# Attention decoder: second-pass scores in pairs of PSUM banks, first-pass scores in a ring of two banks

## The reference, cut to what matters

```python
scores = jnp.einsum('bhqd,bhkd->bhqk', q, k) / math.sqrt(HD)
scores = scores + mask[None]
attn = jax.nn.softmax(scores, axis=-1)
out = jnp.einsum('bhqk,bhkd->bhqd', attn, v)
```

## Time and profile before

| | us |
|---|---|
| median of 3 runs | 2834.61 (2833.82 to 2835.52) |
| the profiled execution's own time | 2834.0 |
| its span in the profile | 2832.2 |
| PE busy in the span | 2383.4 (84%) |
| DVE busy | 1830.1 (65%) |
| ACT busy | 1364.2 (48%) |
| GpSimd busy | 512.9 (18%) |
| mean granted clock of TensorE | 0.906 |

### The profile page before, as it was taken

The page is one execution under the profiler, slowest core; times in us unless marked ns, Lnnn a source line. Parts: engine busy times, 40 slices in busy tenths (PEclk is TensorE's granted clock), DMA queues, the critical chain, the costliest instruction groups (busy, mean ns, idle before and its releaser), DMA issues. The chain is left out here.

```text
span 2832.2 us, 37728 instructions
## 1 busy us (share of the span) xinstructions
PE 2383.4 (84%) x12692; PEld 999.5 (35%) x12692; DVE 1830.1 (65%) x4370; ACT 1364.2 (48%) x2333; POOL 512.9 (18%) x603
## 2 busy tenths in 40 slices
PE   6799999999999999999678798984556987999638
PEld 4333334343434434333243323431122533333215
DVE  3686777777776777777237765358999145877242
ACT  2365666666666666666535123344222612566420
POOL 1211111110111111010014001006896002100000
PEclk7799999999999999999889898986899986999868
DMA  2221222221222222121010000003332012222020
GB/s 91 83 90 43 81 66 69 74 82 53 70 65 79 69 66 81 50 71 54 20 36 1 22 1 27 0 12 120 126 138 100 23 44 69 83 64 74 20 90 15
DMA packets 77451, 171.60 MB, mean 61 GB/s; under 512 B 23049, under 2 KB 38665, under 8 KB 73163
## 3 DMA queue, kind: packets, MB, share of 16 engines
q1 hardware_dynamic: 77258, 169.18, 18.8%
HBM read 128.41 MB, written 39.71 MB: 59 GB/s over the span
## 5 line engine op out<-in xcount | busy, mean ns | idle before, releaser
L1056 ACT ACTIVATE sb_prob<-ps 128x512 f32<-128x512 f32 (+1 forms) x1520 | 805.3, 575 | 483.4 <-PE ps L846 307.9
L820 PE MATMUL ps<-sb_k_stack_half,sb_q_stack_half 78*128 78x512 bf16 (+3 forms) x1920 | 588.1, 340 | 56.2 <-DMA sb_q_stack_half<-q_rows 24.5
L846 PE MATMUL ps<-sb_q_stack_half,sb_k_stack_half 81*128 81x128 bf16 (+2 forms) x2240 | 569.8, 312 | 53.4 <-ACT sb_prob L1056 51.9
L957 DVE TENSOR_REDUCE sb_row_max<-ps 128x1 f32<-128x512 f32 x640 | 431.7, 686 | 140.6 <-PE ps L820 138.8
L966 DVE CUSTOM_DVE_ANT_0 sb_masked_scores<-ps,sb_mask_row,sb_row_max 128x128 bf16<-128x128 f32 (+3 forms) x640 | 341.2, 544 | 93.3 <-PE ps L820 90.0
L966 DVE CUSTOM_DVE_ANT_0 sb_masked_scores<-ps,sb_mask_row 128x128 bf16<-128x128 f32 (+3 forms) x640 | 283.2, 487 | 172.1 <-PE ps L820 171.3
L846 PEld LDWEIGHTS ps<-sb_q_stack_half,sb_k_stack_half 81*128 81x128 bf16 x2240 | 201.8, 99 | 385.6 <-ACT sb_prob L1056 199.2
L867 PE MATMUL ps<-sb_prob,sb_v_first_half 128*9 128x512 f32 (+3 forms) x2560 | 300.3, 542 | 0.2 <-ACT sb_o_raw L1063 0.2
L820 PEld LDWEIGHTS ps<-sb_k_stack_half,sb_q_stack_half 78*128 78x128 bf16 x1920 | 184.4, 100 | 268.7 <-DVE sb_row_max L966 79.4
L2606 PE MATMUL ps<-sb_read_out,sb_ident 128*128 128x512 f32 x256 | 139.6, 678 | 119.7 <-DVE sb_read_out L2693 113.8
L2660 POOL TENSOR_TENSOR sb_inflow<-sb_delta_u,sb_b_spread 128x1024 f32<-128x1024 f32 x64 | 201.4, 3162 | 26.3 <-DVE sb_states L2682 19.0
(11 more groups left out here) (375 smaller groups left out, 3171.6 us busy)
## 6 DMA issues: line engine op xcount, KB each, us to landing
sb_q_stack_half<-q_rows SPq DMA_DIRECT2D x240, 96.0 KB
sb_k_stack_half<-k_rows SPq DMA_DIRECT2D x40, 576.0 KB
o_rows<-sb_o_raw SPq DMA_DIRECT2D x80, 256.0 KB, 2.3
sb_b_spread<-b_rows SPq DMA_DIRECT2D x32, 512.0 KB, 4.7
sb_c_spread<-c_rows SPq DMA_DIRECT2D x32, 512.0 KB, 3.5
sb_k_stack_half<-k_rows SPq DMA_DIRECT2D x40, 288.0 KB
q_rows<-sb_qk_parts SPq DMA_DIRECT2D x60, 128.0 KB, 2.1
k_rows<-sb_qk_parts SPq DMA_DIRECT2D x60, 128.0 KB, 2.1
```

The lines of the kernel that those rows point to most:

```text
L820: pe.matmul(M.ps[:, k % RING, 0:hi - lo], qst[half][0:S1_ROWS, s, j, at:at + P], kst[half][0:S1_ROWS, s, lo // CH, j, 0:hi - lo], start=Tr ...
L846: mm = pe.matmul(bank[:, x * w + lo:x * w + hi], kst[half][0:S2_ROWS, s, t // 4, j, t % 4 * P:(t % 4 + 1) * P], qst[half][0:S2_ROWS, s, j, ...
L957: dve.reduce_max(rowmax[:, tau % 3, 0, at:at + 1], M.ps[:, k % RING, 0:w], AX_X).then_inc(first_done, 1)
L1056: act.activation(prob[:, st % PROB_STEPS, heads[0]:heads[-1] + 1, a:CH], scores.rearrange("p (j q) -> p j q", j=len(heads)), ACT.Exp).then ...
```

## The change

Units are now 2 heads at widths 512 and 384, and 4 heads at 256 and 128. A unit has two banks: one head in each at 512 and 384, two heads in each at 256; at 128 all four lie in the first bank. The second pass has two such pairs, banks 2 and 3, and 4 and 5. The first pass has the two banks 0 and 1. Both rings are now two deep (`RING` is 2). One ACT instruction exponentiates a whole unit.

PE computes a unit head by head, and the pieces that are due are put between the heads, with a mark for each head from `Plan`. The wait for the pair of banks stands before the unit's first head; the signal to ACT comes from its last matmul. A narrow head is one matmul of its whole width, where it was cut into matmuls of 128 columns, and the mask comes after a bank's heads, no longer before them.

```diff
--- before.py
+++ after.py
@@ -382,7 +382,7 @@
     def units_of(self, tau, t):
         half = self.tasks[tau][2]
         width = CH - max(t * P - half * CH, 0)
-        per = {2 * P: 2, P: 4}.get(width, 1)
+        per = 2 if width > 2 * P else 4
         return [tuple(range(j, j + per)) for j in range(0, GROUP, per)], width
 
     def side_items(self, q):
@@ -454,7 +454,7 @@
                 ready[q] = end + items[q][at[q]][1]
             return name, q, norm_of.get(q)
 
-        self.steps = []
+        self.steps, self.marks = [], {}
         now = 0.0
 
         def add(task=None, t=None, units=(), first=(0, 0), cost=0.0):
@@ -507,8 +507,12 @@
             units, width = self.units_of(tau, t)
             lo, rows = k, []
             for u in units:
-                done += (len(u) * width + self.DVE_FIX) / per_group
-                k = target(done)
+                marks = []
+                for _ in u:
+                    done += (width + self.DVE_FIX / len(u)) / per_group
+                    k = target(done)
+                    marks.append(k)
+                self.marks[(tau, t, u)] = marks
                 rows.append(("exp", tau, u, k))
                 rows += [("turn", x[1], None, k) for x in due_turns(k)]
             mask = 0.06 * GROUP if width < CH or t == 4 * self.tasks[tau][2] else 0.0
@@ -637,7 +641,7 @@
     plan = Plan(F.layers, F.ffn, F.rotate, SLOTS)
     col = F.col
     steps, tasks = plan.steps, plan.tasks
-    S2_BANK, RING, O_BANK, SIDE = 3, 3, 6, 7
+    S2_BANK, RING, O_BANK, SIDE = 2, 2, 6, 7
     ROWS = 4 * GROUP
 
     with ExitStack() as tmp:
@@ -825,31 +829,28 @@
                     pe.wait_ge(max_split, plan.splits[tau])
                     if v >= RING:
                         pe.wait_ge(unit_done, v - RING + 1)
-                    pe.matmul(M.ps[0:3 * ROWS, S2_BANK + v % RING, 0:P], m3[:, tau % 2].rearrange("p c r -> p (c r)"),
+                    pe.matmul(M.ps[0:3 * ROWS, S2_BANK + 2 * (v % RING), 0:P], m3[:, tau % 2].rearrange("p c r -> p (c r)"),
                               M.identb[:], start=True, stop=True).then_inc(s2_ready, 1)
 
-                def second(v, tau, t, heads):
+                def second(v, tau, t, heads, x):
                     half, s = tasks[tau][2], plan.slot[tau]
-                    if t == 0 and heads[0] == 0:
+                    if t == 0 and heads[x] == 0:
                         pe.wait_ge(rows_in[half][s], 48 * (plan.use[tau] + 1))
-                    if v >= RING:
+                    if v >= RING and x == 0:
                         pe.wait_ge(unit_done, v - RING + 1)
                     a, w, diag = place(tau, t)
-                    n = len(heads)
-                    bank = M.ps[:, S2_BANK + v % RING, 0:n * w]
-                    if n > 1:
-                        pe.matmul(bank.rearrange("p (j q) -> p j q", j=n)[:, :, 0:P], M.identb[:],
-                                  M.mask_kq[:].unsqueeze(1).to_broadcast([P, n, P]), start=True, stop=False)
-                    for x, j in enumerate(heads):
-                        for lo in range(0, w, P if n > 1 else w):
-                            hi = lo + (P if n > 1 else w)
-                            mm = pe.matmul(bank[:, x * w + lo:x * w + hi], 
-                                           kst[half][0:S2_ROWS, s, t // 4, j, t % 4 * P:(t % 4 + 1) * P],
-                                           qst[half][0:S2_ROWS, s, j, a + lo:a + hi], start=n == 1,
-                                           stop=x == n - 1 and hi == w and (n > 1 or not diag))
-                    if n == 1 and diag:
-                        mm = pe.matmul(bank[:, 0:P], M.identb[:], M.mask_kq[:], start=False, stop=True)
-                    mm.then_inc(s2_ready, 1)
+                    per = CH // w
+                    at, pos = divmod(x, per)
+                    bank = M.ps[:, S2_BANK + 2 * (v % RING) + at, 0:per * w]
+                    mm = pe.matmul(bank[:, pos * w:(pos + 1) * w],
+                                   kst[half][0:S2_ROWS, s, t // 4, heads[x], t % 4 * P:(t % 4 + 1) * P],
+                                   qst[half][0:S2_ROWS, s, heads[x], a:CH], start=pos == 0,
+                                   stop=pos == per - 1 and not diag)
+                    if diag and pos == per - 1:
+                        mm = pe.matmul(bank.rearrange("p (j q) -> p j q", j=per)[:, :, 0:P], M.identb[:],
+                                       M.mask_kq[:].unsqueeze(1).to_broadcast([P, per, P]), start=False, stop=True)
+                    if x == len(heads) - 1:
+                        mm.then_inc(s2_ready, 1)
 
                 def weigh(tau, t):
                     l, b, half, g = tasks[tau]
@@ -925,7 +926,11 @@
                         if kind == "turn":
                             turn(step["units_at"] + x, tau)
                         else:
-                            second(step["units_at"] + x, tau, step["t"], heads)
+                            for y, mark in enumerate(plan.marks[(tau, step["t"], heads)]):
+                                second(step["units_at"] + x, tau, step["t"], heads, y)
+                                while k < mark:
+                                    first(k)
+                                    k += 1
                         while k < upto and step["task"] is not None:
                             first(k)
                             k += 1
@@ -1043,7 +1048,7 @@
                     if tau >= 2:
                         half = tasks[tau - 2][2]
                         act.wait_ge(rows_in[half][plan.slot[tau - 2]], 48 * (plan.use[tau - 2] + 1))
-                    act.activation(turned[:, tau % 2, :], M.ps[0:3 * ROWS, S2_BANK + v % RING, 0:P],
+                    act.activation(turned[:, tau % 2, :], M.ps[0:3 * ROWS, S2_BANK + 2 * (v % RING), 0:P],
                                    ACT.Copy).then_inc(unit_done, 1)
 
                 def weight(v, tau, t, heads):
@@ -1052,9 +1057,15 @@
                     act.wait_ge(s2_ready, v + 1)
                     if heads[0] == 0 and st >= PROB_STEPS:
                         act.wait_ge(pv_done, st - PROB_STEPS + 1)
-                    scores = M.ps[:, S2_BANK + v % RING, 0:len(heads) * w]
-                    act.activation(prob[:, st % PROB_STEPS, heads[0]:heads[-1] + 1, a:CH],
-                                   scores.rearrange("p (j q) -> p j q", j=len(heads)), ACT.Exp).then_inc(unit_done, 1)
+                    bank = S2_BANK + 2 * (v % RING)
+                    if w > 2 * P:
+                        scores = M.ps[:, bank:bank + 2, 0:w]
+                    elif w == 2 * P:
+                        scores = M.ps[:, bank:bank + 2, :].rearrange("p k (j q) -> p (k j) q", j=2)
+                    else:
+                        scores = M.ps[:, bank, :].rearrange("p (j q) -> p j q", j=4)
+                    act.activation(prob[:, st % PROB_STEPS, heads[0]:heads[-1] + 1, a:CH], scores,
+                                   ACT.Exp).then_inc(unit_done, 1)
 
                 def save(tau):
                     act.wait_ge(pv_done, plan.step_index[(tau, plan.kbs[tau] - 1)] + 1)
```

## The result

The changed kernel takes 3013.6 us (median of 4 runs, 2990.5 to 3024.1) against 2834.2 us (4 runs, 2828.1 to 2835.5): **1.062 times as long**, 95% interval 1.058 to 1.067. The profiled execution took 3008.8 us, with a span of 3007.0 where that of before was 2832.2.

The account below looks back on a forecast made before the run. PE, busy 92% of the decoder stages, was taken to set the pace. The terms +175 + 10 + 8 - 28 = +165 us on 2834.0 gave 2999, rounded to 3000 us; the 8-in-10 range was 2880 to 3085.

Parts of the forecast that it names:

- Part 1: First pass: with two banks, a piece waits for DVE's end of piece k-2 instead of k-3; +175 us in all.
- The walk: Three first-pass steps of 512 queries worked through with the new waits for DVE: 1.90 us lost, 0.63 each.
- ACT's pairs: Second-pass exps: one per pair saves ACT 36 us, all beside its idle time, so the program gains 0 us.
- The turn: Second pass: at 19 of 80 turns the pair directly behind waits for the exp of the pair ahead; +10 us.
- `save`: Second step of a task: `weigh` waits for the later copy of sums in 27 of 80 tasks, 0.3 us each; +8 us.
- GELU: Block 0: PE's stops while ACT does GELU shorten at 14 places by 2.0 us each; -28 us.
- The lower end of part 1: Rival: the first pass's order self-corrects and its shorter ring costs only +80 us, total 2904 us; chance 0.15.
- the faster case: Rival: exps set the pace, DVE's delay is absorbed and PE's second-pass waits go, total 2770 us; chance 0.10.
- The clock rival: Rival: many short waits make TensorE's granted clock fall oftener, 70 us more, total 3070 us; chance 0.10.
- The signals: Profile after: idle before pieces up over 100 us, 800 exps, `weigh` inside GELU gaps, time outside decoders within 3 us.

Follow-up runs that it names:

- 2 / 3 kernel: Kernel before with the first-pass ring cut from three banks to two, the second pass keeping three single banks: 3042.1 us, ratio 1.071.
- four singles: Kernel before with two banks for the first pass and four single banks for the second, no pairs: 2998.4 us, ratio 1.056.
- the copies: GELU replaced by a plain copy, in the kernel before (2809.6 us, 0.991) and in the changed kernel (2978.2 us, 1.050).
- half the reducing: DVE reduces half of each first-pass piece and exp has scale 0, in the kernel before (2783.7 us, 0.981) and the changed kernel (2877.2 us, 1.013).

## Why the prediction was right, and where it wasn't

The direction and the size hold: 3013.6 us lie 14 above the forecast of 3000, and +179 us stand against a sum of +165. Point by point:

- **Part 1, +175 us.** The mechanism is shown by the 2 / 3 kernel, in which nothing but this ring is shorter. It lost 202 us (186 to 216), so the term was some 27 us short. The walk's waits came out at 0.61, 1.16, 0.08 and 0.39 us for 0.62, 1.07, 0.07 and 0.32. (The walk lets DVE take P8 at 712.08, though by its own numbers P8 lands at 711.76 + 0.33 + 0.04 = 712.13; with that it gives 0.37.) Its size over the whole program is not separated cleanly from the clock. The stages' 172 us hold both: at a granted clock c the share 2(1 - c) of the time runs at the lower level and at most half of that is lost, so block 0 lost at most 101 us after (0.07 x 1444) and 53 before (0.04 x 1315), block 3 39 and 25. Up to 62 us of the 172 can so be the clock's, and 110 to 172 are waits and what they bring. At the lower end of that the walk's 0.63 us did not arise in each of the 228 steps; the runs don't say in which. Without GELU block 0 grew by 116 us (1278 to 1394) at 0.97 in both kernels, so there next to nothing of the loss is the clock's.
- **ACT's pairs, 0 us.** The time of the exps fell by 59 us (805.3 to 746.5), 36 forecast, all of ACT's by 45, and the program's by none of it: four singles in the same banks take no longer. The Trainium skill (Perfetto Trace Analysis, Optimizing Scalar/DVE Operations) says that larger operations can pay if the engine is saturated. The trace agrees: ACT is busy in 54% of block 0's stage, and the pairs pay nothing.
- **The turn, +10 us.** The 19 turns with a pair directly behind them show 10.4 us of waits for exps, added up from the timeline, 0.1 to 0.85 each.
- **`save`, +8 us.** `weigh` waited for it 3 times, not 27, 1.9 us in all, and moving it gave 6 us within the scatter. It was priced too high; the runs don't say which of its lengths was off.
- **GELU, -28 us.** This is the step that failed: "so 2.3 us are won", added to part 1 as if the two were independent. At the stop they are won (1.03 us of wait for 2.78). Against the 2 / 3 kernel, which has the short first ring and the old second one, the change is 28 us faster and four singles are 44 us faster. Against the kernel before nothing is left: the copies show a net gain of none, or a loss of some 9 us. Both fit if GELU costs more once the first ring is short, and the clock says so. By the same bound GELU's share of low clock in block 0 costs at most 59 us after the change (0.07 x 1444 less 0.03 x 1394) and 15 before it. The 2 / 3 kernel without GELU, which would part the two, was not run. The forecast allowed for "the clock may still fall during the shorter stop" and took 0.3 us for it.
- **The rivals.** The lower end of part 1 (2904) and the faster case fall with the time and with the 2 / 3 kernel. The clock rival came half true: 0.93 where it asked for 0.91 and where 0.95 or more would have killed it. Its mechanism (TensorE: Matmul & The Clock Gate, A second HAM failure mode: psum-queue depth-cycling, in the Trainium skill) fits the lower clock where the ring is short. But the 0.97 in the long middle of block 0, full of such short waits, speaks against it as the only cause, and so do the stages that grew by 63 us (half the reducing) and 116 us (no GELU) at an equal clock. The low level lies at the start, in block 3 and in the separate stretches.
- **Luck.** Part 1 came 27 us dearer than its term, and the rest of the change, the step from the 2 / 3 kernel to the changed one, gave 28 us where +10 + 8 - 28 gives 10. The misses have opposite signs, so part of the closeness of 3000 to 3014 is misses that cancel.
- **The signals.** Idle before pieces grew by 102 us on PE alone, 97 of them waits for DVE. DVE's idle time before its reduces grew, there are 800 exps with pairs at 1.02 us, `weigh` stands in the gap at GELU, and the rest of the program moved by 3 us.

## What to carry to other kernels

When banks are shared out between two streams, ask of each ring how much it holds for its consumer while the producer is away on something else. Here that is `weigh` and the side items, 1 to 2 us, and two pieces are 1.2 to 1.4 us of DVE's work: the third bank is what bridges it, and a fourth one taken from the second pass doesn't pay. A larger instruction on an engine that is not the bound was worth nothing here, and banks spent on it are taken from somewhere. Walking three steps, with the measured durations and the new wait, gave each wait of these steps within 0.1 us before anything ran. A stop that gets shorter is not yet time won: its price, the clock behind it above all, can depend on the other part of the same change, so the two are not simply added.

## What the runs showed of the hardware

- Stretches of 13 to 17 us at the lower clock level with PE shown busy throughout (0.57 over 20 us at 96% busy), some 25 us behind a stop of 1.0 us. Four of them begin behind a wait of 0.51 us and eight matmuls of one column. The kernel before has none in the middle of block 0, and two of 14 us with only `save` moved.
- The granted clock follows small changes of order: block 0's stage reads 0.96 before, 0.92 with rings of 2 and 3, 0.95 with rings of 2 and 4, 0.93 with pairs, 0.94 with only `save` moved. A few hundredths there are tens of us: 0.94 for 0.96 is 4% of 1320 us more at the lower level, of which at most half is lost.
- A reduce of 256 columns takes 424 ns where one of 512 takes 688: twice 424 less 688 leaves 160 ns that don't shrink with the width.
